# A transformer layer on one core: first norm in two halves, loads in another order, tables asked for later

## The reference

```python
def layer(x):                                    # x: 2 x 1024 x 128, 16 heads of 8
    x = x + attention(layernorm(x))              # this stage begins in the part that is changed
    x = x + mixture(layernorm(x))                # 8 experts, top 2, capacity 512, with a fallback
def attention(x):
    q, k, v = heads(x @ Wq + bq), heads(x @ Wk + bk), heads(x @ Wv + bv)
    q, k = q * cos + rotate_half(q) * sin, k * cos + rotate_half(k) * sin
    att = (q @ k.T + rel_bias_table[bucket]) / sqrt(8)     # causal, bucket of i - j
    return softmax(att) @ v @ Wp + bp
```

## Time and profile before

| what | value |
|---|---|
| runs, us | 449.29, 449.31, 443.89 (median 449.29) |
| profiled execution, us | 449.1, its span 447.6 |
| busy in the span | PE 383.8 us (86%), DVE 309.2, POOL 268.4, ACT 223.9 |
| granted TensorE clock, mean | 0.941 of full speed |

### The profile page before, as it was taken

One profiled execution on the slowest core, in us unless ns is written; L12 is line 12 of the kernel. 1 busy time (PEld: TensorE's weight loads), 2 busy tenths in 40 slices (PEclk: granted clock), 3 DMA queues, 4 the chain that ended last, 5 costly groups with the idle time before them and its releaser, 6 DMA issues.

```text
span 447.6 us, 7356 instructions
## 1 busy us (share of the span) xinstructions
PE 383.8 (86%) x2470; PEld 177.6 (40%) x2470; DVE 309.2 (69%) x722; ACT 223.9 (50%) x498; POOL 268.4 (60%) x242
## 2 busy tenths in 40 slices
PE   8885788999999999999989989997878677999810
PEld 2432434444434334444435334432334325566500
DVE  3786787866777876877875998875366548566514
ACT  1650245767666776666677755767741110333200
POOL 7375084578569778558589358779712460166650
PEclk9998999999999999999999999999985678999965
DMA  8596574203705008906005000004600102133118
GB/s 217 113 269 155 104 153 79 34 1 80 174 1 101 11 0 185 292 17 109 2 1 103 8 2 9 14 8 130 213 15 13 36 29 57 52 95 95 47 46 277
DMA packets 30459, 37.45 MB, mean 84 GB/s; under 512 B 4757, under 2 KB 25045, under 8 KB 30101
## 3 DMA queue, kind: packets, MB, share of 16 engines
q1 hardware_dynamic: 24378, 29.91, 27.8%
q0 software_dynamic: 2240, 4.21, 3.1%
q10 hardware_dynamic: 3808, 2.92, 2.3%
HBM read 28.56 MB, written 12.75 MB: 92 GB/s over the span
## 4 chain that ended last, share of the span: by engine, by line
PE 62%; DVE 18%; DMA 5%; POOL 5%; ACT 4%; issue 4%; SPq 1%; DVEq 0%; POOLq 0%; ACTq 0%
PE ps_av L1128 15%; PE ps_st L1099 12%; PE ps_slot L1020 12%; DVE neg_max L1346 7%; PE ps_slot L1024 5%; PE ps_st L1203 3%; PE ps_slot L1213 3%; ACT probs L910 2%; PE ps_slot L1159 2%; POOL probs L732 2%; DMA x_sb<-in_L_attn_x_dram 2%; PE ps_st L1205 2%; PE ps_st L1107 2%; PE ps_av L1205 1%; PE ps_st L1041 1%
## 5 line engine op out<-in xcount | busy, mean ns | idle before, releaser
L910 ACT ACTIVATE probs<-ps_st 128x512 f32<-128x512 f32 (+3 forms) x384 | 168.7, 494 | 102.0 <-PE ps_st L1099 99.8
L1346 DVE TENSOR_REDUCE neg_max<-ps_slot 128x1 f32<-128x640 f32 (+7 forms) x184 | 175.6, 989 | 55.0 <-PE ps_slot L1024 52.9
L732 POOL TENSOR_TENSOR probs<-probs,f_all 128x960 f32<-128x960 f32 (+2 forms) x65 | 123.8, 1904 | 10.3 <-ACT probs L910 5.5
L1020 PE MATMUL ps_slot<-k_stack,q_stack 128*128 128x512 bf16 (+3 forms) x384 | 99.5, 329 | 11.3 <-DVE neg_max L1346 6.3
L1099 PE MATMUL ps_st<-q_stack,k_stack 128*128 128x512 bf16 (+3 forms) x384 | 103.1, 329 | 2.8 <-ACT probs L910 2.5
L1128 PE MATMUL ps_av<-probs,v_all 128*9 128x512 f32 (+3 forms) x768 | 81.2, 497 | 2.1 <-POOL probs L732 1.6
L729 POOL TENSOR_SCALAR_AFFINE_SELECT probs<-probs 128x512 f32<-128x512 f32 x58 | 37.0, 638 | 68.7 <-ACT probs L910 68.5
L1024 PE MATMUL ps_slot<-b_all,flip_b 128*128 128x240 bf16 (+2 forms) x288 | 65.4, 252 | 0.0
L1099 PEld LDWEIGHTS ps_st<-q_stack,k_stack 128*128 128x128 bf16 x384 | 34.5, 97 | 74.0 <-ACT probs L910 54.0
L1020 PEld LDWEIGHTS ps_slot<-k_stack,q_stack 128*128 128x128 bf16 x384 | 35.8, 98 | 44.7 <-DVE neg_max L1346 13.1
L737 POOL DMA_INDIRECT slots<-token_rows,slot_no x32 | 33.2, 1039 | 32.3 <-DVEq L1534 24.4
(11 more groups left out here) (188 smaller groups left out, 403.5 us busy)
## 6 DMA issues: line engine op xcount, KB each, us to landing
q_stack<-q_parts SPq DMA_DIRECT2D x21, 192.0 KB
slots<-in_c_rows_dram SPq DMA_DIRECT2D x4, 528.0 KB, 9.3
probs<-slots SPq DMA_DIRECT2D x8, 264.0 KB, 2.7
parts<-in_c_rows_dram SPq DMA_DIRECT2D x4, 512.0 KB, 9.4
q_stack<-parts SPq DMA_DIRECT2D x4, 512.0 KB, 5.5
k_stack<-k_parts SPq DMA_DIRECT2D x14, 128.0 KB
f_all<-g_vec ACTq DMA_DIRECT2D x1, 1536.0 KB, 11.3
q_parts<-part_all SPq DMA_DIRECT2D x16, 96.0 KB, 3.3
```

The lines of the kernel that those rows point to most:

```text
L732: pool.tensor_tensor(pr, pr, f_of[:, n % (H // HG), :, fo:fo + hi - lo], ALU.mult).then_inc(near_done, 1)
L910: act.activation(probs[:, u % PBUF, g, c0:512], ps_st[:, ST_NO[what] % 3, c0:512], ACT.Exp, scale=SCALE).then_inc(exp_done, 1)
L1020: pe.matmul(ps_slot[:, slot, o + lo:o + hi], q_stack[:, buf, t // MT, g, t % MT * P:(t % MT + 1) * P], k_stack[:, buf, lo // CW, g, 0:hi - ...
L1346: dve.tensor_reduce(neg_max[:, t // MT, heads[0]:heads[-1] + 1, t % MT], src, AX.X, ALU.max, negate=True).then_inc(slot_used, 1)
```

## The change

- `LN` becomes two items. The first handles tiles 0 to 7 whole. The second takes the statistics of tiles 8 to 15 and the guess of their roots on VectorE; GpSimd does their three Newton steps and the bias (14 operations), and ScalarE's `XN 2` and `XN 3`, each in two pieces of two tiles, wait for that.
- The sync queue's loads: x 0, Wq, Wk, x 1, rotary tables of the first 512 tokens, x 2, x 3, rotary tables of the other 512, Wv, Wp. Wq and Wk have a semaphore of their own, and each half of the tables and `bv_row` too; GpSimd's small loads now wait for Wv and Wp.
- The first heads' `f_all` is loaded behind both halves of group 0's stacks; ScalarE's `LOAD` stands after `LO 1 1` and waits for the first half of the stacks.
- `PROLOGUE` has another order; the warming loops have 16 and 8 matmuls.

```diff
-WARM_FIRST, WARM_PROJ, WARM_SLOTS = 24, 10, 8
+WARM_FIRST, WARM_PROJ, WARM_SLOTS = 16, 8, 8
-PROLOGUE = [("LN",), ("XN", 0), ("XN", 1), ("XT", 0), ("VEC",), ("ZERO",), ("XN", 2),
-            ("PROJ", 0, 0), ("XT", 1), ("HI", 0, 0), ("REST", 0, 0), ("PROJ", 0, 1), ("LOAD",), ("MID", 0, 0),
-            ("HI", 0, 1), ("XN", 3), ("REST", 0, 1), ("LO", 0, 0), ("XT", 2), ("MID", 0, 1), ("LO", 0, 1),
-            ("PROJ", 1, 0), ("HI", 1, 0), ("REST", 1, 0), ("PROJ", 1, 1), ("XT", 3), ("MID", 1, 0), ("HI", 1, 1),
-            ("REST", 1, 1), ("LO", 1, 0), ("PROJ", 2, 0), ("MID", 1, 1), ("LO", 1, 1), ("ADD", 2, 0), ("PROJ", 2, 1),
-            ("PROJ", 3, 0), ("PROJ", 3, 1), ("ADD", 2, 1), ("ADD", 3, 0), ("ADD", 3, 1)]
+PROLOGUE = [("LN", 0), ("XN", 0), ("XT", 0), ("XN", 1), ("LN", 1), ("VEC",), ("ZERO",), ("PROJ", 0, 0), ("XT", 1),
+            ("HI", 0, 0), ("REST", 0, 0), ("PROJ", 0, 1), ("XN", 2, 0), ("MID", 0, 0), ("HI", 0, 1), ("PROJ", 1, 0),
+            ("LO", 0, 0), ("XN", 2, 1), ("REST", 0, 1), ("PROJ", 1, 1), ("XN", 3, 0), ("XT", 2), ("MID", 0, 1), ("HI", 1, 0),
+            ("LO", 0, 1), ("XN", 3, 1), ("REST", 1, 0), ("HI", 1, 1), ("PROJ", 2, 0), ("MID", 1, 0), ("REST", 1, 1),
+            ("XT", 3), ("PROJ", 2, 1), ("LO", 1, 0), ("MID", 1, 1), ("LO", 1, 1), ("ADD", 2, 0), ("LOAD",), ("PROJ", 3, 0),
+            ("PROJ", 3, 1), ("ADD", 2, 1), ("ADD", 3, 0), ("ADD", 3, 1)]
...
+            load_x(0)
+            sp.dma_start(w_attn[:, 0, :], Wq[:, :]).then_inc(wqk_in, 16)
+            sp.dma_start(w_attn[:, 1, :], Wk[:, :]).then_inc(wqk_in, 16)
+            load_x(1)
+            load_turns(0)
+            load_x(2)
+            load_x(3)
+            load_turns(1)
+            for i, w in enumerate((Wv, Wp)):
+                sp.dma_start(w_attn[:, 2 + i, :], w[:, :]).then_inc(w_in, 16)
...
             load_tiles(sp, b_all, r_vec, 0, HG, toep_in)
-            load_tiles(sp, f_all, g_vec, 0, HG, factors_in)
...
                 load_k(0, 0, (c,), half_in[c])
+            load_tiles(sp, f_all, g_vec, 0, HG, factors_in)
             for c in range(2):
                 store_parts(c, (1,), next_out)
...
-            pool.wait_ge(w_in, 64)
+            pool.wait_ge(w_in, 32)
             pool.dma_start(router[:, :], Wr[:, :]).then_inc(late_in, 16)
...
+            def late_roots():
+
+                r = slice(TPB, TT)
+                v, t, dst = newton[:, 0, r], newton[:, 1, r], rstd[:, 0, r]
+                pool.wait_ge(late_guess, 1)
+                for _ in range(3):
+                    after(pool.tensor_tensor(t, dst, dst, ALU.mult))
+                    after(pool.tensor_tensor(t, t, v, ALU.mult))
+                    after(pool.tensor_scalar(t, t, -0.5, 1.5, ALU.mult, ALU.add))
+                    after(pool.tensor_tensor(dst, dst, t, ALU.mult))
+                after(pool.tensor_tensor(xn_bias[:, r], mv[:, r, 0], dst, ALU.mult))
+                after(pool.tensor_scalar(xn_bias[:, r], xn_bias[:, r], -1.0, None, ALU.mult))
+                pool.sem_inc(late_bias, 1)
...
-            act.wait_ge(w_in, 64)
+            act.wait_ge(wqk_in, 32)
...
                     act.wait_ge(vec_out, 32)
+                    act.wait_ge(half_in[0], HALF_IN)
                     load_tiles(act, b_all, r_vec, HG, H - HG, toep_rest)
...
+                if h:
+                    root_guess(rstd[:, 0, r], newton[:, 0, r])
+                    dve.sem_inc(late_guess, 1)
```

More of the change, by code:

```diff
@@ L382, in layer_kernel @@
         t_in = sem("t_in")
-        rope_in = sem("rope_in")
+        rope_in = [sem(f"rope_in{h}") for h in range(2)]
+        bv_in = sem("bv_in")
         ones_in = sem("ones_in")
@@ L514, in _, with load_x, load_turns @@
         def _(sp):
-            for c in range(NCH):
+            def load_x(c):
                 sp.dma_start(x_sb[:, c * CH:(c + 1) * CH, :], x_tiles[:, c * CH:(c + 1) * CH, :]).then_inc(x_in[c], 16)
-            for i, w in enumerate((Wq, Wk, Wv, Wp)):
-                sp.dma_start(w_attn[:, i, :], w[:, :]).then_inc(w_in, 16)
-            sp.dma_start(wide[:, 0:2 * T], c_wide[:, 0:2 * T]).then_inc(rope_in, 16)
+            def load_turns(h):
+                half = [w[:, 0:2 * T].rearrange("p (s h c) -> p s h c", s=2, h=2)[:, :, h, :] for w in (wide, c_wide)]
+                sp.dma_start(half[0], half[1]).then_inc(rope_in[h], 16)
+            load_x(0)
[8 more added lines that the diff above has]
+                sp.dma_start(w_attn[:, 2 + i, :], w[:, :]).then_inc(w_in, 16)
             def store_part(c, i, groups, done):
@@ L769, in _ @@
                 kind = what[0]
-                if kind == "RS":
+                if kind == "LN":
+                    if what[1]:
+                        late_roots()
+                elif kind == "RS":
                     if what[1] == 0 and what[2]:
@@ L831, in _, with normalise @@
             act.activation(below_b[:, :], below, ACT.Copy).then_inc(const_b, 1)
-            def normalise(c):
-                for t in range(c * CH, (c + 1) * CH):
-                    act.wait_ge(bias_done, 1)
+            def normalise(c, tiles):
+                for t in tiles:
+                    if c < 2:
+                        act.wait_ge(bias_done, 1)
+                    else:
+                        act.wait_ge(late_bias, 1)
                     act.activation(xn[c][:, t % CH, :], x_sb[:, t, :], ACT.Identity, bias=xn_bias[:, t:t + 1],
@@ L872, in _ @@
                 if kind == "XN":
-                    if what[1]:
-                        normalise(what[1])
+                    c = what[1]
+                    if c == 1:
+                        normalise(c, range(CH, 2 * CH))
+                    elif c:
+                        first = c * CH + what[2] * CH // 2
+                        normalise(c, range(first, first + CH // 2))
                 elif kind == "XT":
@@ L1269, in _, with first_norm @@
             stat_count = [0]
-            def first_norm():
-                for t in range(TT):
+            def first_norm(h):
+                tiles = range(h * TPB, (h + 1) * TPB)
+                for t in tiles:
                     if t % CH == 0:
@@ L1275, in first_norm @@
                     dve.bn_stats(stats[:, t, :], x_sb[:, t, :]).then_inc(st_done, 1)
-                stat_count[0] += TT
-                dve.wait_ge(st_done, TT)
-                for t in range(TT):
+                stat_count[0] += TPB
+                dve.wait_ge(st_done, stat_count[0])
+                for t in tiles:
                     dve.bn_aggr(mv[:, t, :], stats[:, t, :]).then_inc(mv_done, 1)
[L1280 to L1284, removed]
+                dve.wait_ge(mv_done, stat_count[0])
+                r = slice(h * TPB, (h + 1) * TPB)
+                after(dve.tensor_scalar(newton[:, 0, r], mv[:, r, 1], LN_EPS, None, ALU.add))
+                if h:
+                    root_guess(rstd[:, 0, r], newton[:, 0, r])
+                    dve.sem_inc(late_guess, 1)
+                else:
+                    rsqrt(rstd[:, 0, r], newton[:, 0, r], newton[:, 1, r])
+                    dve.scalar_tensor_tensor(out=xn_bias[:, r], in0=mv[:, r, 0], scalar=-1.0, in1=rstd[:, 0, r],
+                                             op0=ALU.mult, op1=ALU.mult).then_inc(bias_done, 1)
             def normalise_first():
@@ L1538, in _ @@
                 if kind == "LN":
-                    first_norm()
+                    first_norm(what[1])
                 elif kind == "XN":
```

13 lines of the change are left out of this document (11 added, 2 removed).

## The result

The change made the kernel slower: 455.56 us median of four runs (455.43 to 456.12), against 449.06 for the kernel before beside it (443.89 to 449.31). The ratio is 1.0175, with a 95% interval of 1.0101 to 1.0249: the loss is clear, its size is anything from 1 to 2.5%. I had forecast 446.9, between 441.5 and 450.3. The profiled execution took 455.43, its span 453.3 against 447.6, with a mean granted clock of 0.938 (0.941 before).

A forecast was written before the change was run, and what follows sets the result against it. It took TensorE's attention stage to set the end, so an earlier front, one thread up to the first maximum, moves everything. Terms -2.0 - 0.9 + 0.5 = -2.4 took the profiled 449.1 to 446.9, range 441.5 to 450.3.

The forecast's parts named there:

- Halved norm: VectorE's front: normalising after the second x chunk gives xn 0 at 13.3, 2.7 earlier; 1.0 reaches the first rotation, at 18.35.
- Roots on GpSimd: GpSimd's front: Wp lands at 14.3 (13.0 to 17.0), roots end at 22.2, first subtraction starts where it did, 22.39.
- What hangs on the late bias: Front behind GpSimd's roots: PROJ 2 and 3 wait for the bias at 22.2; the last rotation ends at 36.8.
- Splits: New order of the q and k splits: q's low part at 25.5 (27.6 before), k's near 29.0 (28.7 before).
- Tables behind the stacks: Stores and stack loads free of table traffic: k's store takes 2.8, first score at 36.3, first maximum at 36.85, 2.0 gained.
- The clock: TensorE at the first scores: a shorter wait avoids the 0.50 clock from 40 to 42; 0.9 gained (0 to 0.9).
- What the moved tables hit: Second half's stores and loads: 2.3 MB issued at 36.3 makes its last k load late; 0.5 lost (-0 to 4).
- the tables collide: Rival: second half, max rows and factors queue behind 2.3 MB, giving back all that is won; 449.3, chance 0.15.
- the gain is absorbed: Rival: before the steady part, a wait that doesn't move (stack load or store of parts) takes the gain; 449.3, chance 0.08.
- W: Theory: Wp lands behind both rotary halves; GpSimd's loads wait for it, roots for the loads, chunks 2 and 3 for roots.
- my first rival: GpSimd is the bound: its loads and roots, 7.9 us, come after Wp; 450.3 with Wp at 18.2, chance 0.12.
- T: Theory: the tables asked for behind the first stacks hold up the second half, the maxima and group 1.

The follow-up runs named there:

- e1: The kernel after with GpSimd's wait for Wv and Wp and its six small loads moved behind its last addition of the front; 453.99 us, ratio 1.0111.
- e2: The kernel after with both table loads back at their old, early places; 453.7 us, ratio 1.0100 to the kernel before.
- e3: The kernel after with the edits of e1 and e2 together: small loads last, tables early; 449.73 us, ratio 1.0015.
- e5: e3 with ScalarE's LOAD (768 and 1536 KB of tables) moved behind the first transposed scores; 464.1 us, ratio 1.0309.
- e8: e3 with the late half's Newton steps and bias on VectorE instead of GpSimd; 450.61 us, ratio 1.0009.
- e13: e2 with the late half's Newton steps and bias on VectorE instead of GpSimd; 450.06 us, ratio 1.0024.
- e7: e2 with Wv and Wp loaded ahead of the rotary tables; 449.17 us, ratio 1.0005 to the kernel before.
- e4: The kernel before with only the two table loads moved late, as in the change; 452.76 us, ratio 1.0081.
- e9: The kernel before with only the other heads' tables (2.3 MB, ScalarE's queue) late, behind the first half of the stacks; 450.27 us, ratio 1.0038.
- e10: The kernel before with only the first heads' f_all (512 KB, sync queue) late, behind both halves of group 0's stacks; 449.81 us, ratio 1.0030.
- e12: e7 with the first heads' f_all late, behind both halves of group 0's stacks; 446.86 us, ratio 0.9960.
- e14: The same kernel as e12, measured again in five rounds; 448.41 us, ratio 0.9978.
- e11: e7 with 24 and 10 warming matmuls; 449.93 us, ratio 1.0013 to the kernel before.
- e6: The kernel before with ScalarE's LOAD moved behind the first transposed scores; 460.58 us, ratio 1.0258.

## Why the prediction was wrong

The direction was wrong and the time lay outside the range; point by point:

- **Halved norm**: right in mechanism. The second chunk of x landed 1.3 later than my 7.9, xn 0 was done at 14.4 instead of 13.3, the first rotation came at 19.14 for 18.35. VectorE was busy ahead of it, as forecast.
- **Roots on GpSimd**: this is the step that failed first. I took 14.3 for Wp, since "the total in front of Wp is the same as was in front of the rope's end". It landed at 17.7, beyond the upper end of 17.0. In the seven profiles with this order of loads (after, e1, e2, e3, e5, e8, e13) it landed between 15.4 and 17.9, every time above my 14.3. Equal bytes ahead are not an equal place: the second rotary half landed at 16.9 here, where the whole table had landed at 14.8, and Wp 0.8 behind it. The issues were held up too (the second rotary half took 1.99 us to issue and Wv 1.21, so Wp was issued at 7.70); how much of the lateness comes from that no run separates. The row to go by was bp_row, the small load issued right behind the rotary tables, at 17.0. The rest of that step was sized well: 3.9 for the loads (18.00 to 21.85), 4.4 for the roots (4.1).
- **What hangs on the late bias**: forecast 22.2 for the roots' end and 36.8 for the last rotation, 14.6 between them; measured 26.35 and 42.58, 16.2. My own prices for a late Wp don't agree with each other: the term's bound has a loss of 0.6 at 17.0, the rival a draw at 17.2, and both were too low. In e2 Wp landed at 16.6, and the first maximum came at 42.63. Against e1, where only the wait and the loads are out of the way, the roots of the kernel after end 4.8 later (26.35 against 21.55) and the last rotation 6.1 later (42.58 against 36.49): all of the lateness comes through, and 1.3 more. The 1.3 is put down to a cold TensorE. It waited for the late bias, and its next projections took 2.07 and 1.92 for 1.1 and 1.0, at a clock of 0.50:

```profile
...
29.69 1.12 PE L1027 MATMUL ps_st<-wide,probs 128*128 128x128 f32 x4 [4.69 <-ACT probs L873]
31.50 2.07 PE L1039 MATMUL ps_slot<-acts,w_attn 128*128 128x512 f32 x2 [0.69 <-ACT acts L881]
33.36 1.92 PE L1040 MATMUL ps_slot<-acts,w_attn 128*128 128x512 f32 x2
...
```

```profile
...
32.00:35.00 3.00, 3.00 (x4) 0.90 (x3) 0.00 (x0) 2.39 (x5) 2.96 (x3) 0.50 0.25 60
...
```

  These are TensorE's timeline and busy time by stretch of the kernel after. The two projections alone lost 1.9; with the full clock and the roots in time the same stretch took 14.9 in e1 and 15.1 in e7. So of the 5.9 by which the first maximum missed its 36.85, 4.15 were there at the roots' end, 1.2 to 1.3 are (as an estimate) the clock, and the rest is my stepping through the queues.
- **Splits**: they follow the roots. q's low part was stored at 29.61 (forecast 25.5), k's at 33.22 (29.05).
- **Tables behind the stacks**: right at the place that I looked at. k's first store took 1.82 us (33.22 to 35.06) where I had taken 2.8, and e4 shows the whole gain at the first maximum: 2.8 by the tables alone.
- **The clock**: the stretch of 0.50 at the first scores went (1.00 from 40 to 44), as forecast, but the same loss returned at 32 to 35.
- **What the moved tables hit**: the second step that failed, by size. I allowed 0.5 lost, 4 at most. e4 lost 7.5 and e1 5.3 behind the first maximum. I had priced one reader, the last load of the second half, and it did stretch (2.94 to 7.46 in e9). I had not priced the readers behind it (the 4 KB of maxima, 1.8 to 7.8 us; group 1's parts behind 512 KB) nor a clock that falls in the new wait. The rival "the tables collide" had the mechanism, with 449.3 as its time because it only gave back what was won; e4 gave back more than twice what the tables won.
- **A row that I read past**: against "the gain is absorbed" I wrote that "in the first 100 us only the thread above waits for DMAs". The same chain of the kernel before has one more wait for a DMA, and it is for the maxima:

```profile
...
69.10 2.72 DMA q_stack<-max_rows
...
```

  In e1 the transfer of the first maxima was the wait on that chain, at 44.55, with 7.07 us.

The Trainium skill, in "DMA: Bandwidth & Descriptors", section "Queues, rings and completion order", says that an engine takes turns between queues by packets. The trace shows more than the doubling that I had drawn from it: 2.5 times for that load in e9, and for the 4 KB transfer 2.8 times (5.1 in e9), or over 4 times with 512 KB ahead of it on its own queue as well (e1, e4).

In the kernel after, the late first maximum (3.9) hides what the moved tables win there, and gives them time to land, so they take 1.6 behind it and not 5 to 7.5. Net, this saves nothing. Counted from e3, which has neither cause, the second turned maxima come 2.5 later in e1, 2.5 later in e2 and 4.9 later in the kernel after: as far as one profile of each can tell, the two causes simply add.

The cases of my list were right, then: W was my first rival and T my second. I gave them 0.12 and 0.15, took them for alternatives, and priced both too low: at Wp's 17.7 the first stands between its 449.3 and 450.3, and the second at 449.3. Both happened, and either alone took the kernel to 454 (453.7 in e2, 453.99 in e1).

## What to carry to other kernels

A load that seems to be needed late is needed as early as the first instruction queued behind its wait. Before moving one, list what stands behind the wait on that engine, and when a step is handed to an "idle" engine, count its idle time from the end of its own waits. For a load moved to the end of a queue, take its landing from the row of the load that stood in that place, not from a sum of bytes. And large transfers that are taken out of the way of one reader should be priced against every reader in the next stage, with TensorE's clock in the new gap: here 2.8 us won at the first maximum cost 7.5 behind it.

## What the runs showed of the hardware

- A transfer of 4 KB on the sync queue took 1.8 us with no large transfer beside it (before, e10), 5.1 with 2.3 MB on ScalarE's queue (e9), and 7.1 to 7.8 with 512 KB ahead of it on its own queue as well (e1, e4).
- The issue of a load took 0.4 to 0.5 us on the sync queue for most, but in the kernel after 1.99 for the eighth of the row (512 KB) and 1.21 for the 64 KB behind it, while the first ones were still under way. In the kernel before the fifth and sixth of the row, 64 KB each, took 1.00 and 0.76.
- The first two projections ran at half speed (about 2.07 and 1.92) in the profiles of e2, e5, e8, e12, e13 and e14 and at full speed in those of after, e1, e3 and e7, all with 16 and 8 warming matmuls. With 24 and 10 they ran at full speed in e11, and in the five profiles of the old order (before, e4, e6, e9, e10). Five of the six executions with the half speed took longer than the median of their kernel, by 0.7 to 4.3 us. One profile of each does not settle whether the ten matmuls prevent it, and e11's time was not lower than e7's.
